# Rotating and splitting the attention queries head by head on GpSimd, with a third buffer for the masked scores

## What is computed

```python
q = _rmsnorm(hidden_states @ Wq_a, q_a_ln_w) @ Wq_b
q_nope, q_pe = (q[..., :NOPE], q[..., NOPE:])
q_pe = _apply_rope(q_pe, cos, sin)          # xp * cos + rotate_half(xp) * sin
scores = jnp.einsum('bhqd,bhkd->bhqk', qf, kf) * scale
probs = jax.nn.softmax(jnp.where(causal, scores, min), axis=-1)
o = jnp.einsum('bhqk,bhkd->bhqd', probs, v)
```

## Time and profile before

| | |
|---|---|
| median of 3 runs | 632.92 us (631.91 to 633.07) |
| profiled execution, its own time | 632.73 us |
| span of its trace | 630.8 us |
| busy: PE, PEld, DVE, ACT, POOL | 590.5, 427.7, 461.4, 400.0, 198.9 us |
| mean granted TensorE clock | 0.984 of full speed |
| granted clock from 60.9 to 64.0 us (pair 0) | 0.50 |
| attention stage, pair 0 | about 45 to 74 us of the span |
| attention stage, pairs 1 to 14 | 25.34 us each, the same pattern every time |

### The profile page before, as it was taken

The page is one execution under the profiler, slowest core; times in us unless marked ns, Lnnn a source line. Parts: engine busy times, 40 slices in busy tenths (PEclk is TensorE's granted clock), DMA queues, the critical chain, the costliest instruction groups (busy, mean ns, idle before and its releaser), DMA issues.

```text
span 630.8 us, 10967 instructions
## 1 busy us (share of the span) xinstructions
PE 590.5 (94%) x3336; PEld 427.7 (68%) x3336; DVE 461.4 (73%) x1235; ACT 400.0 (63%) x1157; POOL 198.9 (32%) x172
## 2 busy tenths in 40 slices
PE   4786999999999999999999999999989999978996
PEld 4675767677677676776776767767658888754564
DVE  5876677677776777777767777777867888878466
ACT  4454677777777677766776777668753545264343
POOL 3134333443344334433353444344000000024630
PEclk9898999999999999999999999999989999999998
DMA  8100212312132122221331213205465000001003
GB/s 316 31 1 16 87 47 89 95 54 71 56 104 78 48 84 76 78 72 52 97 89 48 82 55 101 71 19 153 154 209 226 2 0 2 0 30 50 1 14 121
DMA packets 19561, 46.93 MB, mean 74 GB/s; under 512 B 2608, under 2 KB 3120, under 8 KB 19248
## 3 DMA queue, kind: packets, MB, share of 16 engines
q1 hardware_dynamic: 19504, 46.23, 22.8%
HBM read 39.80 MB, written 6.42 MB: 73 GB/s over the span
## 4 chain that ended last, share of the span: by engine, by line
PE 50%; issue 15%; DVE 15%; POOL 9%; ACT 9%; DMA 1%; POOLq 0%; SPq 0%; DVEq 0%; ACTq 0%
PE bank L1017 11%; PE bank L1019 9%; PE bank L1018 9%; PE bank L1072 7%; PE bank L1060 6%; POOL qrot L325 6%; ACT pr L407 3%; POOL qt_lo L332 3%; PE bank L1087 3%; DVE qswp L664 2%; DVE qrot L669 1%; DVE ss L677 1%; ACT pt L415 1%; DVE dot L865 1%; ACT qt_hi L397 1%
## 5 line engine op out<-in xcount | busy, mean ns | idle before, releaser
L677 DVE CUSTOM_DVE_ANT_0 ss<-bank,cst 128x128 f32<-128x128 f32 (+3 forms) x256 | 124.2, 490 | 95.6 <-PE bank L1019 75.0
L415 ACT ACTIVATE pt<-bank 128x128 f32<-128x128 f32 (+3 forms) x256 | 110.3, 431 | 88.4 <-PE bank L1060 88.3
L325 POOL TENSOR_TENSOR qrot<-qrot,qswp 64x512 f32<-64x512 f32 x64 | 81.9, 1280 | 208.2 <-DVE qrot L669 208.1
L407 ACT ACTIVATE pr<-ss,small 128x128 f32<-128x128 f32 (+3 forms) x256 | 142.4, 556 | 4.2 <-DVE small L677 4.0
L1060 PE MATMUL bank<-ident,pr 128*128 128x128 f32 x640 | 117.1, 281 | 0.6 <-ACT pr L407 0.6
L1017 PE MATMUL bank<-kt_hi,qt_hi 128*128 128x128 f32 (+3 forms) x256 | 101.0, 395 | 7.9 <-DVE small L677 4.5
L1060 PEld LDWEIGHTS bank<-ident,pr 128*128 128x128 f32 x640 | 74.5, 141 | 49.5 <-ACT pr L407 28.8
L332 POOL TENSOR_TENSOR qt_lo<-qrot,qt_hi 128x512 fp32r<-128x512 f32 x64 | 82.0, 1290 | 29.2 <-ACT qt_hi L397 27.9
L1072 PE MATMUL bank<-pt,kvn 128*64 128x256 f32 (+3 forms) x512 | 86.2, 448 | 0.7 <-ACT pt L415 0.7
L1019 PE MATMUL bank<-kt_hi,qt_lo 128*128 128x128 f32 (+3 forms) x256 | 82.9, 324 | 0.0
L1018 PE MATMUL bank<-kt_lo,qt_hi 128*128 128x128 f32 (+3 forms) x256 | 82.7, 323 | 0.0
(11 more groups left out here) (163 smaller groups left out, 1072.5 us busy)
## 6 DMA issues: line engine op xcount, KB each, us to landing
sv<-sv SPq DMA_DIRECT2D x16, 576.0 KB, 5.0
rsb<-rinv_scratch SPq DMA_DIRECT2D x64, 128.0 KB, 2.9
sq<-sq SPq DMA_DIRECT2D x16, 448.0 KB, 3.3
wvo_scratch<-vs SPq DMA_DIRECT2D x16, 256.0 KB, 4.8
wv_raw<-wvo_scratch SPq DMA_DIRECT2D x8, 512.0 KB, 4.8
xa<-x SPq DMA_DIRECT2D x8, 256.0 KB, 5.0
x<-x SPq DMA_DIRECT2D x1, 2048.0 KB, 9.6
out<-yo SPq DMA_DIRECT2D x8, 256.0 KB, 2.0
```

The lines of the kernel that those rows point to most:

```text
L325: nc.gpsimd.tensor_tensor(qrot[RKV:P, h, :], qrot[RKV:P, h, :], qswp[RKV:P, h, :], ALU.add)\
L407: nc.scalar.activation(pr[:, k % 4, 0:n], ss[:, k % 2, 0:n], ACT.Exp, bias=negmax[:, k % 8:k % 8 + 1], scale=-1.0, accum_out=rsum[:, k:k + ...
L415: nc.scalar.activation(pt[:, b, h, 0:i + 1, i * P:(i + 1) * P], bank[2 + k % 2][:, 0:(i + 1) * P].rearrange("p (j q) -> p j q", q=P), ACT. ...
L677: nc.vector.tensor_tensor_reduce(out=ss[:, k % 2, 0:n], in0=bank[k % 2][:, 0:n], in1=mask[:, SEQ - n:SEQ], scale=-SCALE, scalar=3.4e38, op ...
```

## The change

Four edits. GpSimd finishes one query block (addition, then subtraction) before it starts the next. ScalarE copies the first block of each two one step earlier: in step 1 instead of 2 (except in pair 0), directly behind `weights_hi`, and in step 9 instead of 10, ahead of the copy of `vs`. The masked scores have three buffers, in the order RING, and only units 1 and 15 of a pair, whose buffer was used two units before, still wait for the exponential. The third buffer takes the place of 2 KB that were left free, so that the tiles behind it stay where they were.

```diff
+RING = (0, 1, 2, 0, 1, 2, 0, 1, 2, 0, 1, 2, 0, 1, 2, 1)
+BACK = [next(d for d in range(1, 17) if RING[k - d] == RING[k]) for k in range(16)]
...
-    ss = att.take("ss", [P, 2, SEQ])
+    ss = att.take("ss", [P, 3, SEQ])
...
-    att.at += 32 + 4 * QB * 2 * RKV
+    att.at += 32
...
             def body(p, last=False):
                 for b in (1,) if last else (1, 0):
-                    gi = 4 * p + (2 if b else 4)
-                    pool.wait_ge(a.qt_split, gi)
                     for h in range(2):
-                        add_rotated(gi + h, h)
-                    for h in range(2):
-                        query_lo(gi + h, b, h, gi + 2)
+                        gi = 4 * p + (2 if b else 4) + h
+                        pool.wait_ge(a.qt_split, gi)
+                        add_rotated(gi, h)
+                        query_lo(gi, b, h, gi + 1)
...
-                nc.scalar.activation(pr[:, k % 4, 0:n], ss[:, k % 2, 0:n], ACT.Exp, bias=negmax[:, k % 8:k % 8 + 1],
+                nc.scalar.activation(pr[:, k % 4, 0:n], ss[:, RING[k], 0:n], ACT.Exp, bias=negmax[:, k % 8:k % 8 + 1],
...
-                    if k in (2, 4):
-                        h = (k - 2) // 2
+                    if k in ((2, 4) if first else (1, 4)):
+                        h = k // 4
                         query_hi(4 * p + 2 + h, 1, h, None if first else PU * (p - 1) + UNITS + QB * (h + 1))
-                    if k in (10, 12) and not last:
-                        h = (k - 10) // 2
+                    if k in (9, 12) and not last:
+                        h = k // 12
                         query_hi(4 * p + 4 + h, 0, h, PU * p + QB * (h + 1))
...
-                if not first:
+                if BACK[k] == 2 and not first:
                     dve.wait_ge(a.exp_made, U - 1)
-                nc.vector.tensor_tensor_reduce(out=ss[:, k % 2, 0:n], in0=bank[k % 2][:, 0:n], in1=mask[:, SEQ - n:SEQ],
+                nc.vector.tensor_tensor_reduce(out=ss[:, RING[k], 0:n], in0=bank[k % 2][:, 0:n], in1=mask[:, SEQ - n:SEQ],
```

## The result

The changed kernel takes 639.55 us (median of 4 runs, 638.77 to 640.03) against 632.82 (median of 4, 631.91 to 633.07): ratio 1.0116, 95% interval 1.0102 to 1.013. It is 6.7 us slower, inside the range and inside the likeliest case's own range (639.2 to 643.3). Its profiled execution has a time of 639.13 us; the span of its trace is 637.3.

A forecast was written before the change was run, and what follows sets the result against it. TensorE was taken as the bound, busy 25.01 of 25.34 us per steady pair. 632.73 + 10.5 (14 pairs at about +0.75) - 1.5 (pair 0) = 641.7, or 641.8 us beside the median; range 632.0 to 646.0.

The forecast's parts named there:

- likeliest case: Whole kernel: GpSimd's earlier subtraction stops VectorE and the change is slower, 639.2 to 643.3 us; chance 0.64.
- The collision: Steady pairs: GpSimd's `query_lo` starts on top of two `weights_lo` instructions reading two SBUF tiles, so VectorE stands until GpSimd is done.
- the two ends: Steady pair: `rotate_own` 0.99 us late if VectorE's first instruction wins the tie, 1.14 if GpSimd wins; net +0.68 to +0.83.
- 1.3 or 1.4 us together with the gap between them: Steady pair, sign to look for: time of the two `weights_lo` rows on `sq`, instead of 0.6 us.
- Stall 1: TensorE ahead of unit 7's scores, 0.52 us lost per pair; claimed to grow one for one with `weights_lo`.
- stall 2: TensorE ahead of unit 8's scores, waiting for `qt_lo`; claimed to vanish, a gain of 0.31 us per pair.
- Pair 0: First pair: `weights_lo` claimed to end 1.5 us earlier, cutting TensorE's wait from 3.75 to 2.2 us.
- The extra 1.5 us: First pair: possible further saving, 5 x 0.30 us, if TensorE's clock were kept over the shorter gap; none counted.
- copy in step 1's cover: ScalarE: delaying L415 and unit 4's exponential by 0.52 us claimed hidden, cost 0; without cover at most 0.52.
- VectorE keeps GpSimd out: Steady pairs: both `weights_lo` instructions pass unheld, stop under 0.31 us, kernel faster by 5.8 to 626.9 us; chance 0.17.
- The gains and the stop cancel: Steady pairs: VectorE loses only part of GpSimd's instruction, 0.3 to 0.5 us a pair; about 632.7 us; chance 0.07.
- A further wait: Behind the stop: late exponential of unit 5 and second copy break their cover by 0.2 us a pair; 644.6 us; chance 0.08.

The follow-up runs named there:

- `sq` first: Changed kernel with the two `weights_lo` splits that read `sq` put ahead of the two that read a PSUM bank: 626.28 us, ratio 0.9905 to the kernel before.
- ScalarE's steps alone: Kernel before with only the two earlier query copies on ScalarE (steps 1 and 9), old GpSimd order and two buffers: 632.3 us, ratio 1.0011.
- the last two kernels: Changed kernel with weights split in step 3, `sq` first, copy in step 2 except pair 15; with three, then two score buffers: 618.58 and 618.6 us.
- GpSimd's order alone: Kernel before with only GpSimd's addition and subtraction done head by head, ScalarE's copies in their old steps: 634.22 us, ratio 1.0039.

## Why the prediction was right, point by point

- **The collision.** Right, and shown both ways: it is there with 1.27 us where the prediction put it, and it is gone when either the reading changes (`sq` first) or the time (copy in step 2), with 0.97 us a pair.
- **Its size.** The per-pair term was sized a little too high. Of the two ends, 0.99 and 1.14, the first came: VectorE won the tie by 0.01 us, GpSimd stretched by 0.13, and unit 7's scores came 0.97 late. The middle, 0.75 net, should have been 0.67; times 14 that is 1.2 us too much. Which end comes was not known beforehand, and hangs on 0.01 us. The 0.13 that the first end takes off GpSimd's time has no row beside it in the prediction; the second row would give 0.15 (GpSimd ends 1.13 after VectorE's first instruction, where its kind takes 1.28), and 0.15 it was (212.26 to 213.39). The sign of "1.3 or 1.4 us together with the gap between them" doesn't fit the prediction's own ends, which give 1.59 and 1.74 from the first start to the second end; it measured 1.57.
- **Stall 1 rises one for one, stall 2 goes.** Right: +0.97 and -0.30 in every steady pair, and no further wait.
- **Pair 0.** The wait fell by 1.46 us, by 1.5 in the prediction, and the pair by 1.39. The wait is the firm figure of the two. The length of pair 0 scatters from trace to trace at the same wait: with a wait of 3.75 us it was 26.53 us before and 27.51 with ScalarE's steps alone, with 2.90 us it was 25.57 and 27.05 in the last two kernels; the granted clock in it was lower in the longer ones (0.88 against 0.94, 0.87 against 0.93). The extra 1.5 us of the prediction did not come: the five passes behind the wait took 2.30 us in both kernels, at a granted clock of 0.50. That is not a property of the shorter wait: with GpSimd's order alone, and with the copy back in step 2, the wait was 2.30 us and the five passes took 1.27. So the most there is to win is 1.0 us and not 5 x 0.30. Even that didn't reach the pair: with the copy back in step 2 it took 25.18 us, the changed kernel's 25.14, for the passes right behind the five were the slow ones there. What decides when the clock falls stays open.
- **Third buffer, copy in step 1's cover.** Right, at 0 each, by runs of their own.
- **Copy in step 9.** Right for the sum, since the change has it; but its working was incomplete. It was costed as a move that nobody waits for. In fact the new GpSimd order needs it: without it the second addition comes late, for 0.44 us a pair. The prediction looked only at whose subtraction TensorE waits for, not at what is queued behind that subtraction on GpSimd.
- **The sum.** The terms of the change measured 9.33 - 1.39 = 7.9 against 9.0 predicted, and 1.6 us of unchanged code ahead of pair 0 came out shorter in the profiled execution. The medians differ by 6.7. So the forecast of 641.8 was 2.2 us too high; 1.2 of it is the size of the stop, and the rest is not resolved.
- **The rivals.** "VectorE keeps GpSimd out" is wrong here: the stop is 0.98, not under 0.31. It still describes the row at 581.30, as said at the end. "The gains and the stop cancel" needs a partial stop; it was seen only where GpSimd's instruction is cut in two (0.44, and ratio 1.0). "A further wait" did not occur.

## What to carry to other kernels

Before you move work between engines, list which instructions will now run at the same time and which of them read two SBUF tiles; an instruction that is 0.29 us in the profile took 1.27 here when GpSimd got in first, and turning the order of four independent instructions was worth more than the whole loss. When the order on one engine changes, look at every instruction that moves behind another in its queue, not only at the one that was meant to come earlier. And judge a small edit by the period of the steady stage, which repeats to 0.04 us, rather than by the time of one execution.

## What the runs showed of the hardware

- A held VectorE instruction of 0.29 us with two SBUF inputs ends about 0.15 us after the one GpSimd instruction that holds it, whether that is 1.41, 1.27 or half a subtraction (0.87) long. That is its own time less about 0.14, not a fixed lag: the longer one at 569.71, which takes 0.69 where it isn't held, ends 0.56 after GpSimd's.
- Between two such VectorE instructions, one right behind the other, the waiting GpSimd instruction gets in.
- What GpSimd pays when it waits goes by VectorE's instruction: 1.41 against 1.28 when that was the 0.29 us one, but 3.32 in the row at 581.30, beside one of 1.74.
- That row also shows that not every such pair of instructions behaves as the others. It is there in the changed kernel too: GpSimd starts 0.44 ahead of VectorE's large split, and yet VectorE's isn't held and GpSimd's ends 1.14 after it, as if it had begun only then. So it is in all twelve traces, with GpSimd 0.07 to 0.45 us ahead.

```profile
588.13 1.74 DVE L971 TENSOR_TENSOR wd_lo<-wd,wd_hi 128x1536 fp32r<-128x1536 f32 x1
```

```profile
587.69 3.32 POOL L371 TENSOR_TENSOR fs<-fs,gu 88x512 f32<-88x512 f32 x1 [1.23 <-DVE gu L952]
```

No experiment here tried what makes this case different; it stays open.
